# Local transformer: values projected and mixed per head, in place of windows of x and folded output weights

## What is computed

```python
qkv = x @ Wqkv                                # 128 x 3072; x with half its features shifted by a token
q, k, v = jnp.split(qkv, 3, -1)
q = l2norm(q) * qs
k = l2norm(k) * ksc                           # then rotary tables on both
sim = jnp.einsum('bhwie,bhwje->bhwij', bq, bk2) * QK_SCALE
attn = jax.nn.softmax(sim, -1)                # masked; 32 queries x 64 keys per head and window
out = jnp.einsum('bhwij,bhwje->bhwie', attn, bv2)
return out @ Wo                               # then the residual, and layer norm, GEGLU with 341 inner features
```

## Time and profile before

| | us |
|---|---|
| time, median of 3 runs | 5469.85 (5468.95 to 5472.70) |
| time of the profiled execution | 5472.71 |
| its span, first to last instruction | 5471.0 |
| the stage's part of the span | about 1340 to 4720 |

### The profile page before, as it was taken

The page is one execution under the profiler, slowest core; times in us unless marked ns, Lnnn a source line. Parts: engine busy times, 40 slices in busy tenths (PEclk is TensorE's granted clock), DMA queues, the critical chain, the costliest instruction groups (busy, mean ns, idle before and its releaser), DMA issues. The chain is left out here.

```text
span 5471.0 us, 130377 instructions
## 1 busy us (share of the span) xinstructions
PE 4920.5 (90%) x50569; PEld 3357.5 (61%) x50569; DVE 3869.4 (71%) x6444; ACT 3359.2 (61%) x5923; POOL 2658.0 (49%) x1681
## 2 busy tenths in 40 slices
PE   7888566997999999999999999999999999799897
PEld 4444233664677667776777677767776777566543
DVE  5999786775777767776777777767776777477553
ACT  5776323554666666666666666666666666455444
POOL 4777110001566556665666566556665666266200
PEclk8999767998999999999999999999999999899898
DMA  2121000000000100010001000010001000000020
GB/s 84 62 77 62 4 0 7 2 2 26 12 11 11 31 14 11 11 31 11 11 11 31 14 11 11 19 27 11 11 12 31 12 11 11 14 2 2 24 62 20
DMA packets 76241, 113.89 MB, mean 21 GB/s; under 512 B 22496, under 2 KB 53424, under 8 KB 72048
## 3 DMA queue, kind: packets, MB, share of 16 engines
q1 hardware_dynamic: 67744, 110.60, 7.4%
q10 hardware_dynamic: 8256, 0.03, 0.1%
HBM read 70.38 MB, written 2.49 MB: 13 GB/s over the span
## 5 line engine op out<-in xcount | busy, mean ns | idle before, releaser
L2213 POOL TENSOR_TENSOR lt_qk<-lt_qk,lt_rot 128x1024 f32<-128x1024 f32 x384 | 906.7, 2361 | 203.1 <-DVE lt_rot L2577 203.1
L2223 POOL TENSOR_TENSOR lt_prob<-lt_prob,lt_total 128x1024 f32<-128x1024 f32 x192 | 365.1, 1902 | 1084.8 <-DVE lt_total L2599 1084.8
L2218 POOL TENSOR_TENSOR lt_qk<-lt_qk,lt_rnorm 128x1024 f32<-128x1024 f32 x384 | 726.3, 1902 | 109.7 <-ACT lt_rnorm L2453 102.1
L2260 PE MATMUL lt_ps<-lt_w_qk,lt_xs 128*128 128x512 f32 x1536 | 747.2, 610 | 21.3 <-DMA lt_scales<-in_L_scales 11.3
L2312 PE MATMUL lt_ps<-lt_z,lt_fold 128*128 128x256 f32 x3072 | 678.8, 379 | 1.6 <-ACT lt_z L2481 1.6
L2312 PEld LDWEIGHTS lt_ps<-lt_z,lt_fold 128*128 128x128 f32 x3072 | 584.6, 190 | 120.9 <-ACT lt_z L2481 24.7
L2574 DVE TENSOR_TENSOR lt_qk<-lt_ps,lt_table 128x1024 f32<-128x1024 f32 x384 | 468.7, 1221 | 73.9 <-ACT lt_sq L2443 67.0
L2577 DVE TENSOR_TENSOR lt_rot<-lt_ps,lt_table 128x512 f32<-128x512 f32 x768 | 491.3, 682 | 0.0
L2589 DVE TENSOR_REDUCE lt_nmax<-lt_ps 128x16 f32<-128x1024 f32 x192 | 229.5, 1195 | 359.8 <-PE lt_ps L2280 359.8
L2584 DVE TENSOR_REDUCE lt_norm<-lt_sq 128x16 f32<-128x1024 f32 x384 | 464.7, 1210 | 0.0
L2260 PEld LDWEIGHTS lt_ps<-lt_w_qk,lt_xs 128*128 128x128 f32 x1536 | 272.2, 192 | 251.0 <-issue 244.4
(11 more groups left out here) (409 smaller groups left out, 9881.3 us busy)
## 6 DMA issues: line engine op xcount, KB each, us to landing
mb_bs<-mb_rows SPq DMA_DIRECT2D x16, 1536.0 KB, 7.6
lt_xw<-lt_xw SPq DMA_DIRECT2D x192, 128.0 KB
mb_bs<-mb_rows SPq DMA_DIRECT2D x16, 512.0 KB, 4.3
mo_gate_b<-mo_rows SPq DMA_DIRECT2D x16, 512.0 KB, 5.6
lt_xs<-h SPq DMA_DIRECT2D x96, 64.0 KB, 1.9
lt_w_qk<-in_L_ffn_Wqkv SPq DMA_DIRECT2D x6, 1024.0 KB, 5.1
lt_xs<-h SPq DMA_DIRECT2D x96, 63.8 KB, 1.9
lt_wvT<-in_L_wvT SPq DMA_DIRECT2D x6, 512.0 KB, 7.4
```

The source lines that it names most:

```text
L2213: pool.tensor_tensor(qk[:, u, :, :], qk[:, u, :, :], rot[:, u % 2, :, :], ALU.add).then_inc(sg["added"], 1)
L2218: pool.tensor_tensor(qk[:, u, :, :], qk[:, u, :, :], rnorm[:, u, :, :].to_broadcast([P, H, DH]), ALU.mult).then_inc(sg["qk"], 1)
L2260: last = pe.matmul(AT[u][:, 512 * k:512 * k + 512], xs[:, m.j, c:c + P], w_qk[:, a, 512 * k:512 * k + 512], start=True, stop=True)
```

## The change

`turn_x`, the copies lt_xw and their exchange, `weigh`, lt_z and the fold with its input wvT are gone. In their place the values are projected as q and k are: `project_v`, two units per item with a third block of the weights (lt_w_qkv, 1.5 MB a layer for 1 MB). ScalarE copies them to lt_v_tok (token rows), and `values_moved` on SP brings them by 16 transfers into lt_vw, where each window's 64 keys (its own 32 tokens and those before) lie on 64 partitions, once for each half of the heads. `mix` multiplies per head and window a 64 x 64 block of values with 32 columns of the probabilities, on four 64 x 64 tiles of the array; two copies bring it to lt_att, and `attend` applies the plain Wo in 8 matmuls. Wo comes by 8 transfers in `back_weights`. The PSUM regions are assigned anew and the order of all engines moves with them.

Sixteen transfers stand where two stood. The diff, cut to its core:

```diff
-            def other_halves(m):
-                sp.wait_ge(sg["xw"], m.n + 1)
+            def values_moved(m):
+                sp.wait_ge(sg["v_out"], 2 * m.n + 2)
                 sp.sem_inc(sg["fetch_step"], 1)
-                sp.wait_ge(sg["z_made"], 8 * m.n)
+                sp.wait_ge(sg["mixed"], 8 * m.n)
+                sp.sem_inc(sg["fetch_step"], 1)
                 for k in range(2):
-                    sp.dma_start(xw[64 - 64 * k:P - 64 * k, 1, :, :], xw[64 * k:64 * k + 64, 0, :, :]).then_inc(sg["xw_moved"], 16)
+                    for s in range(2):
+                        r = 64 * k + WIN * s
+                        for q in range(4):
+                            w = q + 1 - s
+                            count = 1 if w == 4 else 2
+                            sp.dma_start(vw[r:r + WIN, w:w + 4 * count - 3:4, :, :].rearrange("p w i d -> p w (i d)"),
+                                         v_tok[WIN * q:WIN * q + WIN, 0:count, k, :, :].rearrange("p t i d -> p t (i d)")
+                                         ).then_inc(sg[f"v_moved{k}{s}"], 16)
 
             def front_weights(l):
                 one = bass.ds(l, 1)
-                sp.dma_start(w_qk[:, :, :].rearrange("p a n -> p (a n)"),
-                             T["L1_ffn_Wqkv"][one, :, 0:2 * INNER].rearrange("l p n -> p (l n)")).then_inc(sg["front_in"], 16)
+                sp.dma_start(w_qkv[:, :, :].rearrange("p a n -> p (a n)"),
+                             T["L1_ffn_Wqkv"][one, :, :].rearrange("l p n -> p (l n)")).then_inc(sg["front_in"], 16)
...
-                sp.dma_start(wvT[:, :, :].rearrange("p g n -> p (g n)"), T["L1_wvT"][one, :, :].rearrange("l p n -> p (l n)")).then_inc(sg["fold_in"], 16)
-                sp.dma_start(wo[:, :, :], T["L1_ffn_Wo"][one, :, :].rearrange("l (t p) n -> p (l t) n", p=P)).then_inc(sg["fold_in"], 16)
...
+                heads = T["L1_ffn_Wo"][one, :, :].rearrange("l (j e a d) n -> d e a (l j) n", e=4, a=2, d=DH)
+                for k in range(2):
+                    for a in range(2):
+                        for r, e in ((0, 3 * k), (64, 2 - k)):
+                            sp.dma_start(wo[r:r + 64, k, 2 * a:2 * a + 2, :], heads[:, e, a, :, :]).then_inc(sg["back_in"], 16)
...
+            def project_v(m, t, to):
+                c = WIN + P * t
+                for k in range(2):
+                    last = pe.matmul(to[:, 512 * k:512 * k + 512], xs[:, m.j, c:c + P], w_qkv[:, 2, 512 * k:512 * k + 512],
+                                     start=True, stop=True)
+                last.then_inc(sg["v_proj"], 1)
...
-            def turn_x(m, to):
-                for i, w in enumerate(EARLY):
-                    last = pe.transpose(to[:, P * i:P * i + P], xs[:, m.j, WIN * w:WIN * w + P], core.ident[:, :])
-                last.then_inc(sg["x_turned"], 1)
...
-            def weigh(m, i, to):
-                t, pair = i // 2, i % 2
-                for w in (2 * pair, 2 * pair + 1):
-                    for k in range(2):
-                        r, c = 64 * k, 512 * k + 256 * (w % 2)
-                        copy, i_w = window(4 * t + w, k)
-                        last = pe.matmul(to[:, c:c + 256], xw[r:r + 64, copy, i_w, :],
-                                         probT[r:r + 64, t, :, WIN * w:WIN * w + WIN], start=True, stop=True, tile_position=(r, 0))
...
-            def attend(m, half):
-                for i in range(4 * half, 4 * half + 4):
-                    for k in range(2):
-                        slot = 2 * i + k
-                        last = pe.matmul(attn, fold[:, slot // 8, slot % 8, :], z[:, k, :, i, :], start=(slot == 0), stop=(slot == H - 1))
...
+            def mix(n, t, to):
+                pe.sem_inc(sg["mix_step"], 1)
+                for half in range(0, H // 2, 2):
+                    for w, i, k in itertools.product(range(4), (half, half + 1), range(2)):
+                        r, c = 64 * k, 64 * ((i + k) % 2)
+                        o = 512 * k + P * (i // 2) + WIN * w
+                        last = pe.matmul(to[c:c + 64, o:o + WIN], vw[r:r + 64, 4 * t + w, 2 * (i % 4) + i // 4, :], probT[r:r + 64, t, i, WIN * w:WIN * w + WIN],
+                                         start=True, stop=True, skip_group_check=True, tile_position=(r, c))
+                        if w == 3 and half == H // 2 - 2:
+                            last.then_inc(sg["mixed"], 1)
+
+            def attend(n):
+                for k in range(2):
+                    for j in range(H // 4):
+                        last = pe.matmul(attn, wo[:, k, j, :], att[:, k, j, :], start=(k + j == 0), stop=(k == 1 and j == H // 4 - 1))
+                last.then_inc(sg["attn_out"], 1)
...
             def body(back, front, layer_ends=False):
                 m, n = front, back
                 if m:
-                    project(m, 0)
+                    pe.wait_ge(sg["qkT"], 4 * m.n)
+                    project(m, 0, PT[0])
+                    pe.wait_ge(sg["ffn_h"], m.n - 1)
+                    if not opens(m):
+                        pe.wait_ge(sg["b_up"], m.l + 1)
+                    project_v(m, 0, X3)
                 if n:
-                    pe.wait_ge(sg["s_read"], 2 * n.n + 2)
-                    turn_p(n, 0, X2)
+                    pe.wait_ge(sg["y_ffn"], B + n.n)
+                    turn_p(n, 0, X1)
                 if m:
-                    project(m, 1)
+                    pe.wait_ge(sg["s_read"], 2 * m.n)
+                    project(m, 1, PT[1])
                 if n:
-                    pe.wait_ge(sg["xw_moved"], 32 * n.n + 32)
+                    for k in range(2):
+                        for s in range(2):
+                            pe.wait_ge(sg[f"v_moved{k}{s}"], 64 * n.n + 64)
                     pe.wait_ge(sg["pT"], 2 * n.n + 1)
-                    weigh(n, 0, X2)
-                    weigh(n, 1, X3)
+                    mix(n, 0, X1)
                     if m:
-                        pe.wait_ge(sg["qk_read"], 4 * m.n + 1)
+                        pe.wait_ge(sg["v_out"], 2 * m.n + 1)
                     else:
                         pe.wait_ge(sg["ffn_h"], n.n)
-                    turn_p(n, 1, X1)
+                    turn_p(n, 1, X3)
                 if m:
-                    if n:
-                        pe.wait_ge(sg["z"], 4 * n.n + 1)
-                    project(m, 2)
+                    pe.wait_ge(sg["qk_read"], 4 * m.n + 1)
+                    project(m, 2, PT[2])
                 if n:
                     pe.wait_ge(sg["pT"], 2 * n.n + 2)
-                    weigh(n, 2, X1)
-                    if m:
-                        pe.wait_ge(sg["qk_read"], 4 * m.n + 2)
-                    else:
-                        pe.wait_ge(sg["y_ffn"], B + n.n)
-                    weigh(n, 3, X0)
+                    mix(n, 1, X3)
                 if m:
-                    if n:
-                        pe.wait_ge(sg["z"], 4 * n.n + 2)
-                    project(m, 3)
+                    pe.wait_ge(sg["qk_read"], 4 * m.n + 2)
+                    project(m, 3, PT[3])
                 if n:
-                    pe.wait_ge(sg["z"], 4 * n.n + 4)
-                    attend(n, 0)
-                    attend(n, 1)
+                    pe.wait_ge(sg["back_in"], 16 * BACK * (n.l + 1))
+                    pe.wait_ge(sg["att"], 2 * n.n + 2)
+                    attend(n)
                 if m:
-                    pe.wait_ge(sg["qk_read"], 4 * m.n + 4)
-                    turn_qk(m, 0, X3)
+                    project_v(m, 1, X1)
                 if n:
                     centre(n)
+                if m:
+                    pe.wait_ge(sg["qk_read"], 4 * m.n + 3)
+                    turn_qk(m, 0, X2)
+                if n:
                     var(n)
                 if m:
-                    turn_qk(m, 1, X2)
-                    turn_qk(m, 2, X0)
+                    pe.wait_ge(sg["v_out"], 2 * m.n + 2)
+                    turn_qk(m, 1, X1)
+                    pe.wait_ge(sg["qkT"], 4 * m.n + 1)
+                    turn_qk(m, 2, X2)
                 if n:
                     pe.wait_ge(sg["w_1"], n.l + 1)
+                    if m:
+                        pe.wait_ge(sg["qk_read"], 4 * m.n + 4)
+                    else:
+                        pe.wait_ge(sg["s_read"], 2 * n.n + 2)
                     pe.wait_ge(sg["xn"], n.n + 1)
-                    if m:
-                        pe.wait_ge(sg["qkT"], 4 * m.n + 1)
-                    up(n, 0, X3)
+                    up(n, 0, X0)
                 if m:
-                    scores(m, 0, X2)
+                    scores(m, 0, X1)
+                if n:
+                    up(n, 1, X3)
+                if m:
                     pe.wait_ge(sg["qkT"], 4 * m.n + 3)
-                    turn_qk(m, 3, X0)
-                if n:
-                    up(n, 1, X1)
-                if m:
+                    turn_qk(m, 3, X2)
                     if n:
```

(48 more changed lines are left out.)

130 lines of the change are left out of this document (56 added, 74 removed).

## The result

The changed kernel takes 5889.09 us (median of 4 runs, 5878.08 to 5895.1), the kernel before 5469.4 beside it. The ratio of the times is 1.0762, with a 95% interval of 1.0749 to 1.0775: 7.6% slower. The forecast of 5403 us was wrong, in sign too; what came is the first rival, code that no longer stays resident, at more than twice its price.

What follows compares the result with a forecast made beforehand. PE was taken as the bound. Body savings (-69 us), fold (-17), code at edges (+17) and a larger first load (+2) sum to -67: 5405.7 profiled, forecast 5403 us, factor 1.012, range 5345 to 5610.

Steps and rivals of the forecast that it cites:

- the first rival: Layer loop on PE: code not resident, 10 packets refetched per pass, 172 us more, 5575 us; chance 0.25.
- the forecast's condition that the code stays resident: Layer loop on PE: no instruction packets fetched while it repeats; with `mix` at most 2.15 us, chance 0.50.
- `attend` 3.45, as said: `attend` on PE, per body: 16 passes instead of 32, 3.46 us for 6.91, gain 3.45.
- `project_v` 1.72 per unit, as said: New value projection on PE, per body: two units of 1.72 us each, cost 3.44.
- `mix` 2.00 for 1.92: `mix` replacing `weigh` on PE: 1.92 us per half, 3.84 per body, no change (-0.02).
- the series rival (2.78): `mix` on PE: load and matmul in series, 2.78 us per half for 1.92, +165 us, 5568; chance 0.17.
- The probT and csq waits: PE waits per body for ScalarE's probT copy, 0.34 us, and for lt_csq, 0.47 us: both go.
- the term was taken as 0: Values queued behind weights at layer edges: slack shrinks to about 1 to 2 us, cost 0, bounds 0 to 3.
- The new wait for lt_kT: PE ahead of the second `scores`: a wait of 0.86 us replaces the old one of 0.25.
- "Cost nothing": 16 value transfers per item, 1.97 MB: land with 7 us of slack before `mix`, at no cost.
- The layers' ends: Layer edges: the fold's matmuls and wait go, -17 us; 7 more instruction packets per layer, +17 us.
- the gain of 0.72 us per body: PE per body: work -0.47 us and idle time -0.25 us, -69 us over 96 bodies.

Runs made afterwards that it cites:

- the last pair with two and one: Changed kernel with last turn_qk moved ahead of second `up`, its copy behind GELU, before the table load: two bodies per pass 5734.6 us; one, last body folded in, 5373.28.
- the run with 15 passes: Changed kernel with one body per loop pass and, on all engines but SP, the layer's last body as a 15th pass: 5470.54 us, ratio 1.0 to the kernel before.
- the fastest kernel: Changed kernel, one body per pass, 15 passes; last turn_qk ahead of second `up`, its copy behind GELU, ahead of the table load: 5373.28 us, 0.9817 of the kernel before.

## Why the prediction was wrong

**The step that failed** is the forecast's condition that the code stays resident, for which the sum has no term: fetching in the loop stood at nothing, and the refetch was a rival at 0.25. The count behind that rival was right (10 packets per pass, 11 seen), and so was the way in which it would happen. The argument against it, that an old pass lies over 7 or 8 packets' places and that code fetched ahead had to fit as well, was an inference from a trace in which nothing was fetched: it can't show more than that the old pass fits. The runs put the end between some 1770 and 2030 instructions per pass, and the new pass has 2540. The capacity that the rival quotes from the Trainium skill (Advanced Engine Details and Errata, ISA Cache) is 128 KB. Beside a pass counted at 160 KB it should have made the refetch the likeliest case.

**Its price was mis-sized as well.** The prediction took 0.41 us per packet, 4.1 per pass and 172 us. In the pass above the two bodies take 38.06 and 42.31 us (2191.50 to 2229.56 to 2271.87), 80.4 against 68.4 for two bodies with resident code, 12.0 us. The stops make up about 5.9 of them (`scores` 3.94 and 3.93 us for 1.67 in the run with one body, and 1.39 at the branch), the slower steps behind them the other half (`down` 0.85 and 1.5, `project` 0.84 and 1.85, `project_v` 1.18). Over all passes it is less, 377 us / 42 = 9.0 per pass. The clock wasn't in the sum at all. The price doesn't follow the number of packets: 0.29 us per packet in the old kernel with four bodies, 361 / 455 = 0.79 between the last pair with two and one (591 packets for 136, the folded ends included). Where they are run seems to decide: four bursts of 128 passes in one body (`mix`, `mix`, `scores`, `scores`), and the stop in the last of them. That the engine's fetch falls behind over the four is my reading; no run took it apart, and the run with half of `mix` speaks against it as the whole account: with bursts of `mix` half as long and 9 packets for 11 it paid 5.2 us a body for 4.5 (377 / 84).

**With the code resident** the forecast of 5403 would still have missed: 5512 with one body per pass, 5470.5 with the ends shortened. Term by term, from the runs:
- `attend` 3.45, as said. `project_v` 1.72 per unit, as said. `mix` 2.00 for 1.92: the weight loads lie under the matmuls, and the series rival (2.78) falls. The prediction set the loads of `scores` and `weigh` on one slope and saw no penalty of column tiling in that; two points always lie on a line. The loads of `mix`, 64 columns, are a third: 136 ns on average [PEld of L2314, page of the changed kernel], where the slope gives 132.
- The probT and csq waits are gone, as said. In the loop no wait for lt_vw stands ahead of `mix`: the values land in time. At the layers' edges, where the slack was taken as enough, the run with 15 passes waits for them 7.0 us in all, and the fastest kernel 11.1 us, up to 4.2 at once; the term was taken as 0, with 0 to 3 us at 5 edges as its bounds.
- The new wait for lt_kT: 1.19 for the 0.86 taken. The 0.33 are the two mask passes, which were to lie under the copy; they wait as well, as they did in the kernel before. ScalarE isn't late for the copy. In the run with one body it stands idle until the transposes are done:

```profile
2215.48 1.01 ACT L2465 COPY lt_kT<-lt_ps 128x1024 f32<-128x1024 f32 x1 [0.71 <-PE lt_ps L2286]
```

What helps is to transpose earlier, with the copy not put off behind the table load: 97 us, 1.0 per body.
- `scores`: 1.49 and 1.72 for 1.41 each, 0.39 per body in the fastest kernel, put down at zero. With 4 of 16 transfers 0.26 of that is gone. "Cost nothing" held for their landing in time in the loop, not for what they take from PE meanwhile. Most of the 38 us that the transfers cost in the fastest kernel lies at the layers' ends, though.
- The layers' ends: net 0 was taken (-17 for the fold, +17 for code). Over the stage, from the first `var` to the last, what exceeds 95 bodies of the loop's length is 55 us in the kernel before and 115 in the run with one body, 73 with 15 passes.

From `var` to `var` a body in the loop takes 34.29 us in the kernel before, 34.16 in the run with one body, 33.17 in the fastest kernel and 33.02 with few transfers. So the gain of 0.72 us per body was in truth 0.13, and 1.1 once the wait was taken away, 1.3 with the transfers cut as well. Of the 109 us between the forecast and the 5512, some 57 are the body's missing gain (0.59 x 96) and some 60 the layers' ends, 8 more together than the times show. What stays open: why an idle time lowers the clock in some places and not in others, what the transfers take from PE's bursts, and how far ahead the fetch runs.

## What to carry to other kernels

Count the instructions of a hardware loop on PE before lengthening its body, two per matmul pass: some 1770 in a pass of the loop were free, some 2030 cost 5 us a body (5750.7 less 5214.3, less 1.0 x 96 for the longer `mix`, over 84 bodies in loops). Where small tiles multiply the instructions, unroll less: one body per pass instead of two gave back 377 us at once. And when an edit brings out a wait, look at what its releaser's engine does just before and what it will hold up: with the transposes moved ahead in both cases, the copy ahead of one table load was worth 1.8%, and ahead of GELU it cost 2.3%.
